# Fewer waits and joined stores in a hand-ordered recurrence, attention and MoE kernel: five probability buffers late, and a new order on every engine

## The reference, cut to what matters

```
x = x + layernorm(recurrence(layernorm(x)))          # x: (4, 1024, 256)
    recurrence: p = x @ Ws + bs ; g = sigmoid(x @ Wg + bg)
                s[t] = tanh(p[t] + s[t-1]) ; out[t] = g[t] * s[t]
x = x + layernorm(ffn(layernorm(x)))
    ffn: h = rms(x) ; 16 heads of 16, q and k normalized per head,
         causal softmax(q k^T / 4) v, @ wo (first 64 columns zero), x += ...
         xf = rms(x) ; gate over 4 experts, the two best kept
         x += sum_e wts[e] * expert_e(xf)            # experts of 2 to 4 layers, first 64 columns zero
```

## Time and profile before

| | before |
|---|---|
| median of 3 runs | 1541.07 us (1537.92 to 1541.19) |
| profiled execution | 1536.93 us, of which the span 1535.2 us |
| PE busy | 1417.4 us (92%) |
| DVE, ACT, POOL busy | 71%, 57%, 20% |
| mean granted TensorE clock | 0.962 |

### The profile page before, as it was taken

How to read it: one execution, slowest core, us unless ns; L and a number is a source line. 1 busy time by engine, 2 the same in 40 slices (tenths; PEclk the granted TensorE clock), 3 DMA queues, 4 the chain that set the end, 5 groups by cost and what they waited for, 6 DMA issues and landing times.

```text
span 1535.2 us, 34359 instructions
## 1 busy us (share of the span) xinstructions
PE 1417.4 (92%) x12700; PEld 1138.7 (74%) x12700; DVE 1096.4 (71%) x2916; ACT 877.5 (57%) x2038; POOL 311.9 (20%) x1146
## 2 busy tenths in 40 slices
PE   6945799999999899998999999989999999999997
PEld 3424679887898569876888678866888567984797
DVE  7757557746789867778989677877799568882334
ACT  2544446655776676677575853348432786338842
POOL 3343223332233333333322100001000110001000
PEclk9977689999999899999999999999999999999999
DMA  3474545665567556764666666666657576656554
GB/s 120 133 238 132 156 140 152 209 206 175 161 206 206 174 162 202 232 190 143 186 189 198 196 190 184 202 168 185 199 171 224 171 218 204 203 194 186 172 155 127
DMA packets 244278, 278.58 MB, mean 181 GB/s; under 512 B 37136, under 2 KB 167696, under 8 KB 243856
## 3 DMA queue, kind: packets, MB, share of 16 engines
q1 hardware_dynamic: 244112, 276.39, 59.8%
HBM read 234.18 MB, written 43.45 MB: 181 GB/s over the span
## 4 chain that ended last, share of the span: by engine, by line
PE 69%; DVE 12%; ACT 7%; DMA 4%; issue 4%; POOL 2%; SPq 2%; ACTq 0%; DVEq 0%
PE PS L1337 64%; PE PS L1340 3%; ACT work L1291 3%; PE PS L1426 2%; POOL AD L2002 1%; DVE mx L1801 1%; ACT PX L1223 1%; DMA KT<-ktd 1%; DMA vlx<-vd 1%; DVE st L1619 1%; DMA WB<-wlo_e_w 1%; DVE mxb L1801 1%; POOL work L2009 1%; ACT work L1316 1%; DVE rst L1606 0%
## 5 line engine op out<-in xcount | busy, mean ns | idle before, releaser
L1223 ACT ACTIVATE PX<-AD 128x8 f32<-128x8 f32 x1023 | 219.7, 215 | 248.0 <-POOL AD L2002 246.4
L2002 POOL TENSOR_TENSOR AD<-PX 128x8 f32<-128x8 f32 x1023 | 243.7, 238 | 538.1 <-ACT PX L1223 526.0
L1291 ACT ACTIVATE work<-PS 128x1024 f32<-128x1024 f32 (+1 forms) x312 | 286.3, 958 | 64.6 <-PE PS L1337 63.6
L1801 DVE TENSOR_REDUCE mx<-PS 128x2 f32<-128x1024 f32 (+3 forms) x256 | 256.4, 1019 | 62.7 <-PE PS L1337 62.1
L1337 PE MATMUL PS<-work,vlx 128*32 128x256 f32 (+2 forms) x2816 | 236.2, 378 | 14.6 <-POOL work L2009 5.5
L1337 PE MATMUL PS<-EP,u_e_l 128*128 128x256 f32 x1024 | 194.3, 284 | 1.2 <-DVE EP L1667 1.2
L2009 POOL TENSOR_SCALAR_AFFINE_SELECT work<-work 128x512 f32<-128x512 f32 x96 | 63.5, 672 | 612.2 <-ACT work L1291 612.0
L1316 ACT ACTIVATE work<-PS 128x512 f32<-128x512 f32 x176 | 102.2, 593 | 148.6 <-PE PS L1337 147.8
L1337 PE MATMUL PS<-WB,work 128*128 128x192 f32 x1024 | 182.2, 332 | 1.0 <-ACT work L1316 0.6
L1337 PE MATMUL PS<-EP,WB 128*128 128x256 f32 x640 | 178.5, 279 | 0.0
L1337 PEld LDWEIGHTS PS<-WB,work 128*128 128x128 f32 x1024 | 166.5, 191 | 5.2 <-issue 1.8
(11 more groups left out here) (172 smaller groups left out, 2332.0 us busy)
## 6 DMA issues: line engine op xcount, KB each, us to landing
KT<-ktd SPq DMA_DIRECT2D x112, 512.0 KB, 5.0
WB<-wlo_e_l SPq DMA_DIRECT2D x160, 256.0 KB, 3.8
ktd<-KTs SPq DMA_DIRECT2D x128, 128.0 KB, 2.7
WB<-wlo_e_up SPq DMA_DIRECT2D x64, 256.0 KB, 4.2
WB<-wlo_e_w SPq DMA_DIRECT2D x64, 256.0 KB, 4.0
WB<-wdn_e_down SPq DMA_DIRECT2D x64, 192.0 KB, 2.9
KT<-ktd SPq DMA_DIRECT2D x48, 256.0 KB, 3.8
KT<-ktd SPq DMA_DIRECT2D x32, 384.0 KB, 4.4
```

Of the source, the lines that this page charges most:

```text
L1223: eng.activation(cur, AD[n % 2], ACT.Tanh).then_inc(of(*key), 1)
L1291: eng.activation(pt[:, :, :, q0:L], two("sc", *a).rearrange("p a (l q) -> p a l q", l=2)[:, :, :, q0:L], ACT.Exp).then_inc(of(*key), 1)
L1801: eng.tensor_reduce(o, two("mxm", *a)[:, :, 0:w], AX, ALU.max, negate=True).then_inc(of(*key), 1)
L2002: eng.tensor_tensor(AD[n % 2], PX[c % 2][:, :, :, t], PX[(n - 1) // L % 2][:, :, :, (n - 1) % L], ALU.add).then_inc(of(*key), 1)
```

## The change

- PT, the pool of probability buffers, grows from three to five. The two new ones lie in PX[0], the tile of p for steps 0 to 255 and 512 to 767, and can be used once step 768 has been computed and units 8 to 11 have been gated.
- The wait of PE for all staged stores moves from ptr of unit 0 to sc(0, 0, 0), its first score matmul. A load of low weights (wr) waits for the store of its own piece alone; a down weight for its own copy.
- A kst is one DMA of 512 KB in place of four of 128 KB, with the layout of ktd changed to (B, 128, 8, T) for it: one partition's rows are 32 KB apart in place of 8 KB. A vst is two DMAs in place of four.
- PLACES and STEPS are rewritten in full, and so is WARM: 308 extra matmuls in place of 190. PINNED fixes seven PSUM banks.
- x1l is planned without its dependence on the MoE's gelu.

In the new tables the operations of PE stand at nearly the same steps of the recurrence as before. The score matmuls come in 169 uninterrupted groups in place of 205, the value matmuls in 165 in place of 197 (312 of each in both kernels), and PE changes its array mode 789 times in place of 862, counted over its list with the extra matmuls.

```
 BUFFERS = {"bank": 8, "stage": 4, "xnT": 2, "U": 5, "G": 1, "XR": 2, "HA": 1, "hT": 1, "SQ": 1, "QK0": 1, "QK1": 1,
-           "Vs": 1, "QKP": 1, "KTs": 1, "QT": 2, "KT": 3, "VL": 2, "PT": 3, "AVS": 2, "AO": 1, "TV": 1,
+           "Vs": 1, "QKP": 1, "KTs": 1, "QT": 2, "KT": 3, "VL": 2, "PT": 5, "AVS": 2, "AO": 1, "TV": 1,
            "XF": 2, "EF": 2, "EP": 2, "W": 6, "MB": 2, "mx": 1, "MT": 1, "avbank": 1, "GG": 1}
...
 PLACES = {
...
-    "hout1": (39, 93, 120, 127, 156, 192, 184, 215),
-    "hsv": (99, 107, 146, 147, 149, 157, 173, 220, 195, 217, 216, 224),
-    "pxl": (664, 1224),
...
+    "hout1": (60, 97, 104, 156, 147, 262, 194, 246),
+    "hsv": (103, 101, 139, 157, 141, 150, 176, 263, 180, 284, 282, 302),
+    "pxl": (535, 1276),
...
 WARM = {
-    ("aot", 0): 1, ("aot", 2): 1, ("av", 0, 3, 0): 4, ("av", 1, 0, 0): 6, ("av", 1, 1, 0): 1, ("av", 10, 1, 0): 3,
-        ("av", 2, 1, 0): 2, ("av", 6, 3, 0): 1, ("dn", 11, "e2_l4"): 5, ("dn", 15, "e3_out"): 4, ("dn", 2, "e1_down"): 7,
-        ("dn", 6, "e3_out"): 3, ("gm", 2): 9, ("gm", 7): 1, ("hpx0", 0): 3, ("kt", 0, 0): 7, ("kt", 0, 1): 2,
-        ("kt", 1, 0): 5, ("kt", 4, 0): 3, ("kt", 6, 0): 6, ("mtr", 3): 4, ("mxm", 0, 2): 11, ("mxm", 0, 6): 6,
-        ("mxm", 1, 10): 2, ("mxm", 1, 13): 1, ("mxm", 1, 5): 1, ("mxm", 13, 23): 2, ("mxm", 2, 10): 2, ("mxm", 3, 9): 5,
-        ("mxm", 5, 1): 3, ("mxm", 5, 11): 1, ("mxm", 5, 4): 3, ("ptr", 0): 7, ("ptr", 1): 8, ("ptr", 4): 1, ("qk", 0, 0): 8,
-        ("qk", 0, 1): 2, ("qk", 1, 0): 2, ("qk", 15, 0): 1, ("qk", 8, 1): 4, ("qt", 2, 0): 3, ("qt", 8, 0): 2,
-        ("qtr", 0): 2, ("qtr", 2): 2, ("qtr", 3): 1, ("qtr", 5): 1, ("sc", 0, 1, 0): 1, ("sc", 1, 0, 0): 1,
-        ("sc", 1, 2, 0): 12, ("sc", 12, 0, 0): 1, ("sc", 9, 3, 0): 1, ("up", 0, "e0_up", 0): 4, ("up", 15, "e2_l2", 0): 2,
-        ("up", 8, "e2_l3", 0): 1, ("vm", 2): 1, ("wo", 0): 2, ("wo", 1): 5
+    ("av", 2, 1, 0): 2, ("av", 6, 3, 0): 5, ("dn", 0, "e2_l4"): 3, ("dn", 1, "e0_down"): 2, ("dn", 15, "e3_out"): 4,
+        ("dn", 2, "e1_down"): 1, ("dn", 6, "e3_out"): 2, ("hpx0", 0): 7, ("htr", 0, 0): 16, ("htr", 2, 0): 13,
+        ("kt", 0, 0): 31, ("kt", 1, 0): 6, ("kt", 4, 0): 3, ("kt", 6, 0): 2, ("mgt", 0, 3): 2, ("mgt", 1, 0): 9,
+        ("mgt", 4, 0): 4, ("mtr", 3): 3, ("mxm", 0, 0): 1, ("mxm", 0, 10): 2, ("mxm", 0, 14): 4, ("mxm", 0, 2): 6,
+        ("mxm", 0, 4): 1, ("mxm", 0, 6): 5, ("mxm", 0, 8): 2, ("mxm", 1, 11): 2, ("mxm", 1, 8): 1, ("mxm", 11, 30): 3,
+        ("mxm", 13, 20): 6, ("mxm", 2, 14): 2, ("mxm", 3, 8): 1, ("mxm", 3, 9): 1, ("mxm", 5, 0): 7, ("mxm", 5, 1): 2,
+        ("mxm", 5, 10): 1, ("mxm", 5, 5): 6, ("ptr", 1): 13, ("ptr", 5): 4, ("qk", 0, 0): 14, ("qk", 0, 1): 10,
+        ("qk", 1, 0): 10, ("qk", 2, 1): 1, ("qk", 3, 0): 2, ("qk", 8, 1): 3, ("qt", 1, 1): 6, ("qtr", 0): 17,
+        ("qtr", 1): 20, ("sc", 1, 3, 0): 16, ("sc", 10, 1, 5): 1, ("sc", 7, 2, 1): 4, ("up", 1, "e2_l2", 1): 2,
+        ("up", 10, "e2_l3", 0): 1, ("up", 15, "e2_l2", 0): 2, ("up", 15, "e3_down", 0): 1, ("up", 2, "e1_w2", 0): 1,
+        ("up", 8, "e2_l3", 0): 1, ("wo", 2): 1, ("xtr", 1): 1, ("xtr", 2): 8, ("xtr", 4): 1
+}
+PINNED = {
+    ("gm", 11): 0, ("mgt", 0, 0): 1, ("qt", 11, 1): 2, ("sc", 11, 1, 0): 3, ("sc", 15, 0, 6): 2, ("up", 15, "e1_w1", 0): 5,
+        ("vm", 13): 6
 }
...
                 soon = free[pool]
-                if p == "P2":
+                pin = PINNED.get(k, -1)
+                if p in BANKS and pin in idle and (p == "P1" or pin + 1 in idle):
+                    got[k, p] = [pin, pin + 1][:BANKS[p]]
+                    a = max(soon[i] for i in got[k, p])
+                elif p == "P2":
                     a, i = min((max(soon[i], soon[i + 1]), i) for i in idle if i + 1 in idle)
...
                 dma(("hsv", n, gate), 512, (f"hout{gate}", n))
-    add("pool", ("ident",), 1.4)
-    add("pool", ("consts",), 6.6, ("ident",))
+    gated = (*[("pgate", 2 * B + b) for b in range(B)], ("sadd", 3 * L))
+    split = tuple(("wsp", w) for w in PIECES)
+    add("pool", ("ident",), 1.4, take={"PT": gated, "EF": split})
+    add("pool", ("consts",), 6.6, ("ident",), take={"PT": gated, "EF": split})
...
         add("dve", ("pgate", u), 0.6, ("gl", u), last)
-        over = [("htr", 2 * NCH - 1, 3), ("hpx1", 2 * NCH - 1)] if u < BUFFERS["U"] else []
-        if u == 0:
-            over += [("hsv", n, 1) for n in range(8)] + [("hsv", n, 0) for n in range(4, 8)]
+        over = [("htr", 2 * NCH - 1, 3)] if u < BUFFERS["U"] else []
         add("pe", ("ptr", u), 0.354, ("pgate", u), *over, mode="128", take={"P1": (("pcp", u),), "U": (("ost", u),)})
...
         add("act", ("vc", u), 0.48, ("vm", u), ("consts",))
-        dma(("vst", u), 332, ("vc", u), n=4)
+        dma(("vst", u), 332, ("vc", u), n=2)
         add("dve", ("qrs", u), 2.56, ("qred", u, 0), ("qred", u, 1))
...
             add("act", ("kc", u, s), act(1024), ("kt", u, s))
-            dma(("kst", u, s), 512, ("kc", u, s), n=4)
+            dma(("kst", u, s), 512, ("kc", u, s))
             add("dve", ("qq", u, s), 0.8, ("kh", u, s), ("kt", u, s), take={"QKP": (("qt", u, s),)})
...
+        staged = [] if u else [("hsv", n, 1) for n in range(8)] + [("hsv", n, 0) for n in range(4, 8)]
         for g in range(4):
...
                 mask = c == 0 and kb == u // 2
-                add("pe", ("sc", u, g, kb), (0.45 if c == 0 else 0.18 if r == 1 else 0.236) + (0.5 if mask else 0), ("kts", u, g, kb // 4), ("mtd", u),
+                add("pe", ("sc", u, g, kb), (0.45 if c == 0 else 0.18 if r == 1 else 0.236) + (0.5 if mask else 0), ("kts", u, g, kb // 4), ("mtd", u), *(staged if g == kb == 0 else ()),
                     seq=before("sc"), mode="64", take={"P2": (("ex", u, g, kb),), "PT": (("av", u, g, kb),)})
...
         def weights(name, h, k, until):
-            dma(("wr", u, name, h, k), 256 if name in UPS else 192, *([("wst", w) for w in PIECES] if "wr" not in prior else []),
-                *([] if name in UPS else [("wdd", name)]), seq=before("wr"), take={"W": (until,)})
+            dma(("wr", u, name, h, k), 256 if name in UPS else 192, ("wst", (name, h, k)) if name in UPS else ("wdd", name), seq=before("wr"), take={"W": (until,)})
             prior["wr"] = (u, name, h, k)
...
-        dma(("x1l", u), 256, ("x1st", u), ("gel", u, "e2_l3", 1), take={"XR": (("fin", u),)})
+        dma(("x1l", u), 256, ("x1st", u), take={"XR": (("fin", u),)})
         add("dve", ("fin", u), 4.11, ("da", u, "e3_out"), ("x1l", u))
...
             return 32
-        return {"vst": 64, "kst": 64, "mtd": 32}.get(key[0], 16)
+        return {"mtd": 32, "vst": 32}.get(key[0], 16)
...
-        PT = [piece(1024 * i, 1024).rearrange("p (a l q) -> p a l q", a=2, l=2) for i in range(3)]
+        PT = [*[PX[0][:, i].rearrange("p b t -> p (b t)") for i in range(2)], *[piece(1024 * i, 1024) for i in range(3)]]
+        PT = [p.rearrange("p (a l q) -> p a l q", a=2, l=2) for p in PT]
         AVS = [piece(3072 + 256 * i, 256) for i in range(2)]
...
         gd = dram("gd", (NCH, 128, 2, B, L))
-        ktd = dram("ktd", (B, 4, 128, 2, T))
+        ktd = dram("ktd", (B, 128, 8, T))
         x1d = dram("x1d", (B, NCH, 128, 2, C))
...
                     u, n, h, k = a
-                    if n not in UPS:
-                        sp.wait_ge(*done("wdd", n))
-                    for w in PIECES:
-                        sp.wait_ge(*done("wst", w))
+                    sp.wait_ge(*(done("wst", (n, h, k)) if n in UPS else done("wdd", n)))
                     for x in freed(key, "W"):
...
                     (b0, t), _ = tiles_of_time(*a)
-                    for g in range(4):
-                        dst = vd[b, g, :, 2 * c:2 * c + 2, :] if c else vd[b0:b0 + 2, g, :, t, :].rearrange("b p n -> p b n")
-                        eng.dma_start(dst, Vs[:, :, 4 * NV * g:4 * NV * g + VG]).then_inc(of(*key), 16)
+                    for s in range(2):
+                        dst = vd[b, :, :, 2 * c + s, :] if c else vd[b0 + s, :, :, t, :]
+                        src = bass.AP(Vs.tensor, Vs[:, s, :].offset, [Vs.ap[0], [4 * NV, 4], [1, VG]])
+                        eng.dma_start(dst.rearrange("g p n -> p g n"), src).then_inc(of(*key), 16)
                 elif kind == "kst":
...
                     sp.wait_ge(*done("kc", *a))
-                    for g in range(4):
-                        eng.dma_start(ktd[b, g, :, :, 128 * t:128 * t + 128],
-                                      plain(KTs[:, 2 * g:2 * g + 2, :])).then_inc(of(*key), 16)
+                    eng.dma_start(ktd[b, :, :, 128 * t:128 * t + 128], plain(KTs)).then_inc(of(*key), 16)
                 elif kind == "ktm":
...
                         for i, (b, _) in enumerate(tiles_of_time(u)):
-                            eng.dma_start(plain(keys_of(kt[:, 512 * i:], 2, n)), ktd[b, g, :, :, 0:n]).then_inc(of(*key), 16)
```

(20 more changed lines are left out.)

160 lines of the change are left out of this document (80 added, 80 removed), and 490 rows, old and new, of tables (PLACES, STEPS).

## The result

The changed kernel takes 1488.29 us (median, 1483.40 to 1492.91) beside 1539.49 us for the kernel before, ratio 0.9669 with the interval 0.9633 to 0.9705. It is 51 us faster, and the forecast was 25.7 us; the range began at 1502. The profiled execution took 1492.91 us, the longest of its four, with a span of 1491.2 us; that of before took 1536.93. So the two traces differ by 44 us, and that is the sum they can explain.

The account below looks back on a forecast made before the run. PE was taken to set the pace over most of the span, losing time to idle stretches, low clock and changes between matmuls. Terms 2.8 + 1.9 + 10 + 11 = 25.7 us off 1541.1 gave 1515.4, stated as 1516 us, range 1502 to 1541.

Parts of the forecast that it names:

- the rest of the order: PE's other reordered operations, only 22 moved over five places: small stalls come and go, nothing, plus or minus 5 us.
- The wait for staged stores: At ptr 0 in the head: with the wait moved to the first score, ptr 0 starts earlier; 2.8 us, range 0 to 5.5.
- What is late next is the gating: Ahead of ptr 0: the gating waits for step 127; its place in the order makes the gain 0 to 5.5 us.
- Joined stores: Key store on the head's chain: one DMA issue for four frees SP before the key loads; 1.9 us, range 0 to 4.
- the single store lands later by what it was issued earlier: Case for the 512 KB key store in the head: its later landing cancels the earlier issue, so nothing is gained.
- The clock of the head: Between ptr 1 and first score: 95 more extra matmuls bring full clock to the saturated stretch from 180.5 us; 10 us, range 0 to 13.
- that the clock falls all the same: Rival for the head: the 10 us are lost and fillers at half clock cost up to 7; 1530 us, chance 0.20.
- Larger groups: Scores and values, nearly all behind step 768: 36 and 32 fewer groups save PE 11.0 us; at most 14.6, at least nothing.
- groups do not pay: Rival for the late part: PE's saved drain becomes waiting for ACT; 1527 us, chance 0.14.
- gelus pushed back: Rival: on ACT, gelus behind longer groups of exps come later by one exp, 0.96 us; up to 1553 us, chance 0.08.
- 11 us less between the recurrence's end and the end: Sign of success behind the recurrence: fewer, longer groups and 11 us less until the kernel ends.
- Low weights: Loads of low weights (wr) in the head: cost and gain nothing, hidden under unit 0's projection and transposes.

Follow-up runs that it names:

- e8: All code edits of the changed kernel, with the order tables and extra matmuls of the kernel before: 1536.54 us, ratio 0.9965 to the kernel before.
- e3: Changed kernel with the extra matmuls of the kernel before up to step 340, order and banks unchanged: 1500.02 us, ratio 0.9728 to the kernel before.
- e9: Kernel before, in its old order, with the changed kernel's numbers of extra matmuls up to step 340: 1544.67 us, ratio 1.0014 to the kernel before.
- e1: Changed kernel's code, with its order and extra matmuls up to step 340 and the old ones behind: 1515.16 us, ratio 0.9843 to the kernel before.
- e2: Changed kernel's code, with its order up to step 768 and the old order behind, five probability buffers kept: 1507.55 us, ratio 0.9782 to the kernel before.
- e4: Kernel before with only the wait for staged stores moved from ptr 0 to the first score: 1538.71 us, ratio 0.9995 to the kernel before.
- e5: Changed kernel with key and value stores split in four again, new ktd layout kept: 1499.22 us, ratio 0.9708 to the kernel before.
- e6: Kernel before with only the joined stores and the new ktd layout, order untouched: 1531.85 us, ratio 0.9916 to the kernel before.
- e15: Changed kernel with stores split in four, 28 extra matmuls ahead of the first scores and 5 ahead of the first values: 1497.16 us, ratio 0.9693.
- e13: The changed kernel run again, unchanged: 1490.43 us, ratio 0.9654 to the kernel before.
- e14: Changed kernel with 10 extra matmuls ahead of the first scores and 5 ahead of the first values: 1491.68 us, ratio 0.9653 to the kernel before.
- e11: Changed kernel with 84 extra matmuls behind step 768 that cut groups of scores in two: 1527.02 us, ratio 0.9913 to the kernel before.
- e10: Changed kernel with 50 extra matmuls ahead of ptr 0, 14 ahead of the mixing's first scores, 5 to 10 at six later places: 1500.64 us, ratio 0.9732.
- e16: Changed kernel with 20 extra matmuls ahead of ptr 0 and 8 ahead of the mixing's first scores: 1494.10 us, ratio 0.9668 to the kernel before.
- e12: Changed kernel with 84 extra matmuls behind step 768 placed where they change no tile form: 1504.05 us, ratio 0.9762 to the kernel before.

## Why the prediction was wrong, point by point

**The step that failed is the rest of the order: "Stalls of under 2 us each will go and come in both directions: nothing, plus or minus 5."** Only 22 of PE's operations move by more than five places, and I read from that that order has no sum of its own. The head in three steps, at step 340: all code edits with the old order 269.2 to 268.1 (e8), the new order with the old extra matmuls 252.3 (e3), the new extra matmuls 243.2. The order is 15.8 of the 26 us, by single profiles. Part of that is clock: between e8 and e3 the time at half clock fell from 75.5 to 51.2 us between steps 127 and 340. The pair e9 and e1 leaves the clock and the extras out, and there the new order with its code edits still takes 156.4 us for 171.0, 14.6 less, 8 or more of them the order's. By the ratios, e8 to e1 (order and extras of the head) is 19 us, 9 of them the extras. What the order does can be seen: in e8 step 127 is there at 96.3 us, but the gating stands behind weight splits and starts at 99.8; in e3 it starts at 95.2, right behind its step (94.9). ptr 0 and ptr 1 start at 96.0 and 105.2 for 100.6 and 112.7. DVE's list was moved, and I had looked at PE's. No run moved DVE's list alone, so how much of the order's gain is this one move isn't shown. The middle adds to it: 4.5 us in the profile of after, 7.8 in e2's (342.4 for 334.6), where nothing that PE waits for has more than 2.8 us in all on either side. It is spread thin.

**The wait for staged stores, 2.8 us.** The mechanism is as forecast, ptr 0 at 0.15 us behind its gating. The value is not: alone it gives nothing (e4, 0.9976 to 1.0015), as gating and ptr 1 come later there. "What is late next is the gating" was the right sentence; the term should have been the lower end, 0, for the edit. The sooner gating, 6.4 us, needed terms of its own: 3.6 come with order and code (95.2 in e3 for 98.8), 2.8 with the extras (92.4 in after).

**Joined stores, 1.9 us.** On SP as forecast, one issue of 0.5 us for 2.5 to 2.9. Second store to first key load went from 4.84 to 3.80 us, but with the same order on SP it is 3.47 split (e5) and 3.80 joined (after): the case "the single store lands later by what it was issued earlier" came true. The one store lands after 4.0 us in the median, the four after 2.7 each. The estimate of a gain of 1.0 us from the Trainium skill (DMA: Bandwidth & Descriptors, section "Anatomy of one DMA — SWDGE (gpsimd) path") is not borne out either: the page's fit is for DMAs that GpSimd issues, and by it the one store would land after 3.2 us (an estimate), where 4.0 was measured. At the end of the kernel the edit was worth 10 to 13 us (e6) and some 6 (e5 and e15, intervals overlapping), beyond the upper end of 4. The mechanism that the term named is not what pays. A part goes through the clock in the head: e15, with full clock behind the first scores, has step 340 at 244.3 us where e5 has it at 251.8. But its median is only 2 us below e5's. Another part may be the new layout of ktd, which got no price and with which the key loads of 512 KB land 0.6 to 0.7 us sooner. Most of it is open.

**The clock of the head, 10 us.** The total is near, 9.1 us at step 340 from e3 to after, 11.7 in the median, 9 by the ratios, but in part by luck: 3.1 of the 9.1 are there at step 127, by extras ahead of the head's stages (htr, hpx0), which the term left out. Behind step 127 it is 6.0 us, less than the 8.3 by which the profiles of one and the same head differ there. The clock from 100 to 200 us is 0.92 (0.85 or more was asked for), the saturated stretch ran at full clock but for 3.4 us in this execution, and 0.37 us for each one less at half clock (e13 and e14), times 30.7, is 11. But the gain hangs on the order: in the old one it is nothing from step 127 to 340 and nothing in the median (e9). The rival, that the clock falls all the same, had 0.20; the profiles of e1, e11 and e13, with the head of after, show it. The rule of the Trainium skill against idle gaps (TensorE: Matmul & The Clock Gate, section "Why this matters for your kernels") agrees in direction with e14 beside e13. e10, e16 and e9 bound it: where PE waits for others, a filled gap bought nothing.

**Larger groups, 11 us.** Right: 13.5 us less from step 768 on, 17 by the ratios of e2 and after. The price was 0.20 us for a group of scores and 0.12 for one of values; e11 and e12 give 0.10 to 0.14 for each change of form, so 73 changes fewer make 7 to 10 us. Scores and values keep PE busy for 15.0 us less, and PE waits 3.4 less in front of them (11.8 and 8.4 us in the whole part behind step 768); other work of PE took some of it back. So the term is of the right kind, and its closeness to 13.5 is partly chance. (The rival without it, 1541.1 - 14.7, is 1526 and not 1527; nothing hangs on it.) PE's waits for exps and gelus did not grow (2.6 to 2.4 us and 0.4 to 0.2 behind 800 us), so the rivals "groups do not pay" and "gelus pushed back" are out. "11 us less between the recurrence's end and the end" was a poor mark: that is 25.5 us less (707.3 to 681.8), since more of the units' work now lies before step 1023.

**Low weights, 0.** Nearly: PE waits 2.0 us in all for loads of low weights (1.7 the longest), 1.4 before. The relaxed wait was not tried alone; in e8, with all code edits in the old order, it can't be told apart.

**The sum.** Measured in the profiles 26 + 4.5 + 13.5 = 44, forecast 14.7 + 0 + 11 = 25.7. The clock and the groups hold within a few us each, the moved wait gives nothing and the stores more than forecast by another way; 11 of the 18 us that are missing are in the head, and the order, with the clock that it holds, is what had been priced at zero. The 7 us more that the medians show beside the profiles are in the choice of executions: after's was its longest of four, before's below its median.

## What to carry to other kernels

A new order is not the sum of its edits. List for every engine, not only for the one that bounds, what stands ahead of the first operation on the chain (here DVE's weight splits ahead of the first gating), and price the move as a term; here an edit that removed one of two waits ending 3 us apart was worth nothing until the other moved. Extra matmuls belong into the wait just ahead of a saturated stretch, counted at their price in place (0.24 us each at full clock, 0.45 at half) and from the moment at which they can start, so that they end inside it; in a wait whose end another engine sets, early in a chain, they bought nothing here. Even in the right place they showed in the profile and the spread (e14), not in the median. Where executions of one kernel spread by 1%, compare their mean clocks before reading a cause from one profile.

## What the runs showed that had not been expected

- The same code had 3.4 or 24 us at half clock in the same place (after and e13), and 7 us at step 340 go with it (243.2 and 250.6). The length of the wait in front doesn't tell which comes.
- One extra matmul alone costs 0.17 to 0.19 us late in the kernel (e12), less than one of a row of them (0.24). Put into a group of scores it costs 0.20 to 0.27 us more (e11).
- Between steps 127 and 340, 40 us less at half clock were worth nothing in the old order (e9: 171.0 us for 170.9), and 24.7 us less were worth 9.2 in the new one (e14 beside e13).
- With the new layout of ktd the key loads of 512 KB land after 4.2 to 4.4 us in place of 4.9 to 5.0, also with split stores (e5).
